# Attention stages computed with a second, turned score product in place of transposed probabilities

## The chip, the cores and the metric

The kernel runs on one core of one Trainium2 chip. The metric is the device time of one execution in microseconds. Lower is better.

## The reference, cut to what matters

The program is four layers, each a cross attention and a feed-forward part, over x of 64 sequences of 128 rows and 128 features; keys and values come from a context of 120 rows a sequence. The last layer has a self attention besides. All attention has 16 heads of 8 features. Written for one of them:

```python
h = layernorm(x)
q, k, v = (h @ Wq + bq) * 8 ** -0.5, ctx @ Wk + bk, ctx @ Wv + bv   # split into 16 heads
scores = einsum("bqhd,bkhd->bhqk", q, k)                            # masked in a2, a3 and s3
attn = softmax(scores, axis=-1)
x = x + einsum("bhqk,bkhd->bqhd", attn, v) @ Wo + bo
```

## The kernel before

x stays in on-chip memory through all stages. `build` runs them one after another, each with a barrier at its end: a0, f0, a1, f1, a2, f2, a3, a renormalisation, s3, f3. Stages a are cross attentions, s3 is the self attention (128 keys of its own rows, where the others have 120), f are feed-forward. `attention_phase` makes all attention stages. The change touches a1, a2, a3 and s3, which are its `packed` form. a2, a3 and s3 have a mask, a1 has none.

A stage handles 16 groups (NG) of four sequences (GB). A group has S = 16 slots, and in each slot one unit: four heads of one sequence. Each engine runs its own list of slots, with semaphores between them, and what a slot does is written out by hand: TensorE's slot s makes the scores of unit s, the transposes of unit s-2 (TURN), the values of unit s-4 (VALUES), and every fourth slot an output product. The projections for the next group stand in slots of this one (`slot_of`). `groups_loop` writes out the first group, turns a loop over pairs of groups, and writes out the last.

For a unit:
- `scores` (L772 to L794): one product, 96 rows of stacked queries (three terms: high, high and low part, in fp32r) as weights, 480 (or 512) columns of masked keys KM moving. With a mask, a bf16 product of the identity with the mask adds it (L792).
- `softmax_shift` on VectorE: the maximum over keys (L547), then scores minus maximum into PR (L552).
- `exponentials` on ScalarE: exp of PR in place (L704).
- `turn` on TensorE: four transposes of PR into TP (L801), which `turned` on ScalarE copies to PT (L710).
- `values` on TensorE (L825): keys are now in rows, and 16 small products in a layout of 32 columns give four heads' sums with V (VM) and their denominators (DM), into ND. VectorE takes reciprocals (L560) and normalises (L566), TensorE multiplies by Wo (L839), VectorE adds to x (L575).

For a group: `high_part` (ScalarE) and `low_part` (GpSimd, L459) split q and k. SP's queue stacks them with 24 copies within on-chip memory (L398, L404), and `masked_keys` (GpSimd, L348) spreads the stacked keys over the four heads of a unit with zeros elsewhere.

The few names that the prediction uses: PJ is the accumulator of the projections, SC of the scores, TP of the transposes.

## Time and profile before

| | |
|---|---|
| median of 3 runs | 4263.11 us (4260.68 to 4274.32) |
| profiled execution, its own time | 4260.05 us |
| its span, first to last instruction | 4258.2 us |
| TensorE, VectorE, ScalarE, GpSimd busy | 83%, 79%, 55%, 37% |
| mean granted clock of TensorE | 0.897 |
| stage a1, from its first instruction | 549.5 to 1031 us |
| stages a2 and a3 | 1377.6 to 1901.9, 2494 to 3003 us |
| stage s3 | 3034 to 3598.9 us |

Engines in the rows: PE is TensorE, PEld its loading of weights, DVE VectorE, ACT ScalarE, POOL GpSimd, SP the queue that issues most copies. Products are pipelined: a row's duration of 0.27 us for a product of 128 columns holds its latency, and the next one starts earlier than it ends. What a product costs is therefore read from the distance between starts. A row's busy share is that of its engine in the stretch. `<-` names what ended an idle time; "issue" means nothing that the profile shows.

### The profile page before, as it was taken

The page shows a single profiled execution, that of the slowest core. Times are in us where ns is not written, and L with a number is a line of the kernel's source. Part 1 is how long each engine was busy: PE and PEld are TensorE (multiplying, and loading weights), DVE is VectorE, ACT ScalarE, POOL GpSimd, SP SyncE. Part 2 cuts the span into 40 slices and gives each one's busy share as a digit, 9 for nine tenths or more (in the row PEclk, how much of TensorE's full clock was granted, in tenths as well). Part 3 has the DMA queues.
Part 4 walks back from the last instruction along what each step waited for, and adds up shares of the span by engine and source line. Part 5 has one row for each costly group of instructions (what it writes and reads, how often), then busy time and mean ns, then how long its engine had stood idle before and what let it go on. Part 6 is the DMA issues. An engine that isn't in the chain of part 4 may idle for free. (4 is left out here: it accounts for less than half of the span.)

```text
span 4258.2 us, 95393 instructions
## 1 busy us (share of the span) xinstructions
PE 3539.6 (83%) x31830; PEld 2463.6 (58%) x31831; DVE 3346.6 (79%) x6141; ACT 2332.4 (55%) x4244; POOL 1570.1 (37%) x911
## 2 busy tenths in 40 slices
PE   6983979999599899993058849999499998799999
PEld 3552646667476566662046626666365666677777
DVE  7888879998898788885035578888687877788888
ACT  2432657775376566651035536777566665466665
POOL 2210045553000454533744435554254443222222
PEclk9985989998699899995579969999699999799999
DMA  1002122222000222220112142221221112100000
GB/s 63 16 31 103 76 61 64 62 65 63 13 0 6 63 60 57 60 69 13 52 56 62 57 123 62 58 60 49 69 50 47 46 47 73 40 13 12 15 15 15
DMA packets 158984, 209.04 MB, mean 49 GB/s; under 512 B 37820, under 2 KB 109824, under 8 KB 155585
## 3 DMA queue, kind: packets, MB, share of 16 engines
q1 hardware_dynamic: 150593, 189.40, 16.4%
q0 software_dynamic: 8192, 16.92, 1.2%
q8 instruction: 132, 2.16, 0.2%
q14 instruction: 67, 0.55, 0.0%
HBM read 53.09 MB, written 42.21 MB: 22 GB/s over the span
## 5 line engine op out<-in xcount | busy, mean ns | idle before, releaser
L704 ACT ACTIVATE a_p<-a_p 128x480 f32<-128x480 f32 x832 | 501.8, 603 | 517.7 <-DVE a_p L552 515.2
L348 POOL TENSOR_TENSOR a_km<-a_k,a_slots 96x1920 fp32r<-96x1920 f32 x186 | 631.9, 3416 | 176.9 <-DMA a_k<-a_kh 176.9
L547 DVE TENSOR_REDUCE a_mx<-a_sc 128x4 f32<-128x480 f32 (+1 forms) x832 | 542.6, 652 | 124.4 <-PE a_sc L792 95.1
L552 DVE TENSOR_TENSOR a_p<-a_sc,a_mx 128x480 f32<-128x480 f32 x832 | 531.4, 639 | 18.8
L710 ACT ACTIVATE a_pt<-a_tp 120x512 f32<-120x512 f32 x832 | 487.7, 586 | 81.6 <-PE a_tp L801 76.6
L801 PE MATMUL a_tp<-ident,a_p 128*120 128x128 f32 x3328 | 509.7, 276 | 4.1 <-ACT a_p L704 2.3
L801 PEld LDWEIGHTS a_tp<-ident,a_p 128*120 128x120 f32 x3328 | 399.6, 138 | 90.0 <-ACT a_p L704 27.5
L786 PE MATMUL a_sc<-a_km,a_qr 96*128 96x480 f32 x768 | 395.1, 514 | 32.3 <-DMA a_qr<-a_ql 29.4
L825 PE MATMUL a_nd<-a_pt,a_vm 120*32 120x128 f32 x6656 | 354.6, 285 | 0.0
L825 PE MATMUL a_nd<-a_pt,a_dm 120*32 120x128 f32 x6656 | 334.4, 273 | 0.0
L1767 ACT ACTIVATE f_s<-f_pu 128x512 f32<-128x512 f32 x256 | 153.4, 599 | 212.6 <-PE f_pv L1249 212.6
L547 DVE TENSOR_REDUCE s_mx<-s_sc 128x4 f32<-128x512 f32 x256 | 176.4, 689 | 98.1 <-PE s_sc L792 97.5
L560 DVE RECIPROCAL a_rd<-a_nd 128x128 f32<-128x128 f32 x256 | 242.6, 948 | 6.7 <-PE a_nd L825 6.5
L348 POOL TENSOR_TENSOR s_km<-s_k,s_slots 96x2048 fp32r<-96x2048 f32 x62 | 224.0, 3633 | 52.2 <-DMA s_k<-s_kh 52.2
L704 ACT ACTIVATE s_p<-s_p 128x512 f32<-128x512 f32 x256 | 161.2, 630 | 146.3 <-DVE s_p L552 144.8
L1653 POOL TENSOR_TENSOR f_ya<-f_ya,f_yg 128x512 f32<-128x512 f32 x96 | 125.0, 1302 | 302.4 <-DVE f_yg L1703 302.3
L1678 DVE TENSOR_TENSOR f_a<-f_s,f_pv 128x512 f32<-128x512 f32 x256 | 175.3, 685 | 76.2 <-ACT f_s L1767 68.6
L1690 DVE TENSOR_TENSOR f_al<-f_a,f_ah 128x512 fp32r<-128x512 f32 x256 | 229.2, 895 | 0.0
L786 PEld LDWEIGHTS a_sc<-a_km,a_qr 96*128 96x128 f32 x768 | 146.0, 190 | 137.6 <-issue 128.8
L825 PEld LDWEIGHTS a_nd<-a_pt,a_vm 120*32 120x32 f32 x6656 | 131.2, 108 | 141.6 <-issue 132.3
L2078 PE MATMUL f_px<-ident,f_xr 128*128 128x128 f32 x128 | 25.0, 328 | 226.1 <-DMA f_xr<-dispatched 226.1
L825 PEld LDWEIGHTS a_nd<-a_pt,a_dm 120*32 120x32 f32 x6656 | 199.1, 110 | 0.0
(429 smaller groups left out, 8911.6 us busy)
## 6 DMA issues: line engine op xcount, KB each, us to landing
a_qr<-a_qh SPq DMA_DIRECT2D x384, 64.0 KB, 2.0
a_k<-a_kh SPq DMA_DIRECT2D x384, 60.0 KB, 2.0
a_ctx<-in_ctxT SPq DMA_DIRECT2D x64, 240.0 KB, 2.7
a_qr<-a_ql SPq DMA_DIRECT2D x192, 64.0 KB, 2.0
a_k<-a_kl SPq DMA_DIRECT2D x192, 60.0 KB, 2.0
dispatched<-f_empty SPq DMA_DIRECT2D x8, 1040.0 KB, 21.1
f_xr<-dispatched SPq DMA_DIRECT2D x32, 260.0 KB, 2.6
chosen<-f_none SPq DMA_DIRECT2D x8, 1024.0 KB, 11.9
```

Source lines behind the costliest of these rows:

```text
L348: v.tensor_tensor(KM[par][:, i, :, :].rearrange("p b (j k) -> p b j k", k=KN), K3[:, i, :, :].unsqueeze(2).to_broadcast([TR, GB, 4, KN]), ...
L547: v.tensor_reduce(mx[:], view, AX.X, ALU.max).then_inc(mx_ready, 1)
L552: v.tensor_tensor(PR[s % 4][:].rearrange("p (h k) -> p h k", k=k), view, mx[:].unsqueeze(2).to_broadcast([P, heads, k]), ALU.subtract).the ...
L560: v.reciprocal(RD[:], ND[bt % 2][:, 1, :]).then_inc(rd_ready, 1)
L704: a.activation(PR[s % 4][:], PR[s % 4][:], ACT.Exp).then_inc(exp_ready, 1)
L710: a.activation(PT[s % 4][0:KN, :], TP[s % 2][0:KN, :], ACT.Copy).then_inc(pt_ready, 1)
L786: last = t.matmul(SC[s % 2][:, 0:W], queries, keys, start=True, stop=not masked)
L801: last = t.transpose(TP[s % 2][0:KN, q * P:(q + 1) * P], PR[s % 4][:, q * KN:(q + 1) * KN], R.ident[:])
L825: last = t.matmul(ND[j % 2][32 * q:32 * q + 32, what, :], w, PT[s % 4][0:KN, q * P:(q + 1) * P], start=(what == 0 and i == 0), stop=(i == ...
L1678: v.tensor_tensor(A[s % 2][:], S[s % 2][:], PV[s % 2][:], ALU.mult).then_inc(Z["a_ready"], 1)
L1690: v.tensor_tensor(AL[s % 4][:], A[s % 2][:], AH[s % 4][:].bitcast(F32), ALU.subtract).then_inc(Z["lo_ready"], 1)
L1767: a.activation(S[s % 2][:], PU[s % 2][:], ACT.Silu).then_inc(Z["s_ready"], 1)
```

## The change

Stages a1, a2, a3 and s3 are made by a new function. For a unit the scores are formed twice. The first pass, with queries in rows, is only for the maximum: four products, one a head, each with 96 rows of masked queries QM as weights and 120 (128) columns of stacked keys KS moving. VectorE takes the maximum of each (into MX, 16 columns a sequence). Once a sequence, TensorE transposes MX, VectorE negates it into NEG, and ScalarE's queue copies NEG into row 96 of QM. The second pass has keys in rows: KS with a row of ones as 97th is the weights, and QM with the row of minus the maximum is moving, 512 columns, so that the product is score minus maximum and already turned. ScalarE takes exp from the accumulator ST straight to PT. Masked stages add the mask in both passes, in the second from its transpose `addm_t`. The subtraction, the transposes of probabilities and the copy of these are gone.

Keys are no longer masked; queries are (`masked_queries`). The stacking goes by way of memory: high and low parts are written there (`part_out`), and each of the three terms is read back in one copy (`stack_up`). The lags between slots are longer (second pass 9, values 11, output 14 slots behind the first), three groups are written out ahead of the loop, and SP's list is written out whole. Projections stand in slots 2, 4, 6 and 10.

```diff
+def turned_attention_phase(nc, R, I, name, wq, wk, wv, wo, bq=None, bk=None, bv=None, bo=None, own_keys=False, mask=None,
+                           causal=None, ln=None):
...
+    TR = 3 * 32
+    KR = TR + 1
+    U = 4
+    S = GB * U
+    LN_SLOTS = (0, 0, 0, 1)
+    SUM_SLOT, STATS_SLOTS = 14, (15, 15, 15, 15)
+    TURN, NEGATE, WEIGH, VALUES, RECIP, OUTPUT = 5, 6, 9, 11, 12, 14
+    KN = P if own_keys else KC
+    W = 4 * KN
+    steps_of = ["ht", "q", "k", "v"]
+    slot_of = dict(zip(steps_of, (2, 4, 6, 10)))
...
+        KS = [sb(n_(f"ks{i}"), [KR, U, GB, KN], F32R) for i in range(2)]
+        QS = sb(n_("qs"), [TR, U, GB, P])
+        QM = [sb(n_(f"qm{i}"), [KR, GB, U, 4, P], F32R) for i in range(2)]
...
+        MX = [sb(n_(f"mx{i}"), [P, 16]) for i in range(2)]
+        NEG = [sb(n_(f"neg{i}"), [16, P], F32R) for i in range(2)]
...
+        SC = [ps(n_(f"sc{i}"), [P, 512]) for i in range(2)]
+        ST = [ps(n_(f"st{i}"), [P, 512]) for i in range(2)]
...
+                def part_out(step, g, par, which, part):
+                    buffer = R.parts[step][par, which, :, 0:part.shape[1]]
+                    sp.dma_start(buffer, part[:].bitcast(F32)).then_inc(parts_out[step], 16)
+                def stack_up(step, g, par, out, cols_of, order):
+                    sp.wait_ge(parts_out[step], 32 * (g + 1))
+                    for term, which in enumerate(order):
+                        src = R.parts[step][par, which, :, 0:cols_of].rearrange("(i r) c -> r i c", r=32)
+                        sp.dma_start(out[32 * term:32 * term + 32], src).then_inc(stack_in[step], 16)
+                def stack_terms(g, par):
+                    sp.wait_ge(high_ready["q"], g + 1)
+                    part_out("q", g, par, 0, HIGH["q"])
+                    sp.wait_ge(low_ready["q"], g + 1)
+                    part_out("q", g, par, 1, LOW["q"])
+                    sp.wait_ge(high_ready["k"], g + 1)
+                    part_out("k", g, par, 0, HIGH["k"])
+                    sp.wait_ge(low_ready["k"], g + 1)
+                    part_out("k", g, par, 1, LOW["k"])
+                    at_least(sp, qm_ready, g * GB)
+                    stack_up("q", g, par, QS[:].rearrange("p i b t -> p i (b t)"), GT, (0, 0, 1))
+                    at_least(sp, st_ready, (g - 1) * S)
+                    stack_up("k", g, par, KS[par][:].bitcast(F32).rearrange("p i b k -> p i (b k)"), W, (0, 1, 0))
...
+                for g in range(NG):
+                    if not own_keys and 1 <= g < NG - 1:
+                        ctx_load(g + 1, (g + 1) % 2)
+                    stack_terms(g, g % 2)
...
+                def masked_queries(g, par, b):
+                    at_least(pool, st_ready, (g - 2) * S + (b + 1) * U)
+                    nc.gpsimd.tensor_tensor(QM[par][0:TR, b, :, :, :],
+                                            QS[:, :, b, :].unsqueeze(2).to_broadcast([TR, U, 4, P]),
+                                            slots[:].unsqueeze(1).unsqueeze(3).to_broadcast([TR, U, 4, P]),
+                                            ALU.mult).then_inc(qm_ready, 1)
+                def prepare(g, par):
+                    low_part("q", g)
+                    low_part("k", g)
+                    pool.wait_ge(stack_in["q"], 48 * (g + 1))
+                    for b in range(GB):
+                        masked_queries(g, par, b)
+                prepare(0, 0)
+                groups_loop(pool, lambda g, par, first, last: None if last else prepare(g + 1, 1 - par), 3)
...
+                def maxima(g, s):
+                    n = g * S + s
+                    j, i = s // U, s % U
+                    dve.wait_ge(sc_ready, n + 1)
+                    if i == 0:
+                        at_least(dve, mt_ready, g * GB + j - 1)
+                    v.tensor_reduce(MX[j % 2][:, 4 * i:4 * i + 4], SC[s % 2][:, 0:W].rearrange("p (h k) -> p h k", k=KN), AX.X,
+                                    ALU.max).then_inc(mx_ready, 1)
...
+                def negated(b, bt):
+                    dve.wait_ge(mt_ready, b + 1)
+                    if not isinstance(b, int) or b >= 2:
+                        dve.wait_ge(neg_in[bt % 2], (b - bt % 2) * 8)
+                    v.tensor_scalar(NEG[bt % 2][:], ND[(bt + 1) % 2][0:16, 2, :], -1.0, None, ALU.mult).then_inc(neg_ready, 1)
...
+                def negated_in(b, bt, par):
+                    act.wait_ge(neg_ready, b + 1)
+                    act.dma_start(QM[par][TR:KR, bt, :, :, :].rearrange("p i j t -> p (i j t)").bitcast(F32),
+                                  NEG[bt % 2][:].bitcast(F32)).then_inc(neg_in[bt % 2], 16)
+                def exponentials(g, s):
+                    n = g * S + s
+                    act.wait_ge(st_ready, n + 1)
+                    at_least(act, pv_done, n - 3)
+                    a.activation(PT[s % 4][0:KN, :], ST[s % 2][0:KN, :], ACT.Exp).then_inc(exp_ready, 1)
+                def behind(g, s, par, first):
+                    if s - WEIGH < S and not (first and s < WEIGH):
+                        exponentials(g, s - WEIGH)
+                    u = s - NEGATE
+                    if u % U == 0 and u < S and not (first and u < 0):
+                        negated_in(g * GB + u // U, (u // U) % GB, par if u >= 0 else 1 - par)
...
+                def scores(g, s, par):
+                    n = g * S + s
+                    j, i = s // U, s % U
+                    if i == 0:
+                        pe.wait_ge(qm_ready, g * GB + j + 1)
+                    if s == 0:
+                        pe.wait_ge(stack_in["k"], 48 * (g + 1))
+                    at_least(pe, mx_ready, n - 1)
+                    if masked:
+                        t.matmul(SC[s % 2][:, 0:W], R.ident_bf[:], addm[:].unsqueeze(1).to_broadcast([P, 4, KN]), start=True,
+                                 stop=False, skip_group_check=True)
+                    for h in range(4):
+                        last = t.matmul(SC[s % 2][:, h * KN:(h + 1) * KN], QM[par][0:TR, j, i, h, :], KS[par][0:TR, i, j, :],
+                                        start=not masked, stop=True, skip_group_check=True)
+                    last.then_inc(sc_ready, 1)
+                def weigh(g, s, par):
+                    n = g * S + s
+                    j, i = (s // U) % GB, s % U
+                    if i == 0:
+                        b = g * GB + s // U
+                        pe.wait_ge(neg_in[j % 2], (b + 2 - j % 2) * 8)
+                    at_least(pe, exp_ready, n - 1)
+                    last = t.matmul(ST[s % 2][0:KN, :], KS[par][:, i, j, :],
+                                    QM[par][:, j, i, :, :].rearrange("p h t -> p (h t)"), start=True, stop=not masked)
+                    if masked:
+                        last = t.matmul(ST[s % 2][0:KN, :], R.ident_bf[0:KN, 0:KN],
+                                        addm_t[0:KN, :].unsqueeze(1).to_broadcast([KN, 4, P]), start=False, stop=True)
+                    last.then_inc(st_ready, 1)
+                def values(g, s, par, last):
+                    n = g * S + s
+                    j, i = (s // U) % GB, s % U
+                    if s % S == 0:
+                        pe.wait_ge(ready["v"], g + s // S + 1)
+                    pe.wait_ge(exp_ready, n + 1)
+                    if i == 0:
+                        at_least(pe, ct_ready, g * GB + s // U - 1)
+                        if not (last and s // U == GB - 1):
+                            pe.wait_ge(neg_ready, g * GB + s // U + 2)
+                    for what in range(2):
+                        for q in range(4):
+                            h = 4 * q + i
+                            w = DM[0:KN, i, :] if what else VM[par][0:KN, j, 32 * h:32 * h + 32]
+                            last = t.matmul(ND[j % 2][32 * q:32 * q + 32, what, :], w,
+                                            PT[s % 4][0:KN, q * P:(q + 1) * P],
+                                            start=(what == 0 and i == 0), stop=(i == U - 1), skip_group_check=True,
+                                            tile_position=(0, 32 * q))
+                    last.then_inc(pv_done, 1)
+                def maxima_turn(b, bt):
+                    pe.wait_ge(mx_ready, b * U + U)
+                    at_least(pe, ct_ready, b - 2)
+                    t.transpose(ND[(bt + 1) % 2][0:16, 2, :], MX[bt % 2][:], R.ident[:]).then_inc(mt_ready, 1)
...
+                def behind(g, s, par, first, last):
+                    if s - WEIGH < S and not (first and s < WEIGH):
+                        weigh(g, s - WEIGH, par if s >= WEIGH else 1 - par)
+                    if s - VALUES < S and not (first and s < VALUES):
+                        values(g, s - VALUES, par if s >= VALUES else 1 - par, last)
+                    u = s - TURN
+                    if u % U == 0 and u < S and not (first and u < 0):
+                        maxima_turn(g * GB + u // U, (u // U) % GB)
+                    u = s - OUTPUT
+                    if (u + 1) % U == 0 and u < S and not (first and u < 0):
+                        gg = g if u >= 0 else g - 1
+                        output(gg, g * GB + u // U, (u // U) % GB)
...
+                def group(g, par, first, last):
+                    for s in range(S):
+                        scores(g, s, par)
+                        behind(g, s, par, first, last)
+                        if not last:
+                            for step in steps_of:
+                                if slot_of[step] == s:
+                                    project(step, g + 1, 1 - par)
+                    if last:
+                        for s in range(S, S + OUTPUT):
+                            behind(g, s, par, False, True)
...
+        R.parts = {w: nc.dram_tensor(f"parts_{w}", [2, 2, P, GT], F32).ap() for w in "qk"}
...
-        attention_phase(nc, R, I, "a1", I["L1_xattn_wq"], I["L1_xattn_wk"], I["L1_xattn_wv"], I["L1_xattn_wo"],
-                        I["L1_xattn_bq"], I["L1_xattn_bk"], I["L1_xattn_bv"], I["L1_xattn_bo"])
+        turned_attention_phase(nc, R, I, "a1", I["L1_xattn_wq"], I["L1_xattn_wk"], I["L1_xattn_wv"], I["L1_xattn_wo"],
+                               I["L1_xattn_bq"], I["L1_xattn_bk"], I["L1_xattn_bv"], I["L1_xattn_bo"])
...
```

a2, a3 and s3 are called in the same way. The parts left out set up tiles, projections, evictions, reciprocals and the sum into x, as before in kind.

## Rows read from the trace of the kernel before

**Rows 1.** Busy time by stretch, a1 and a3: from:to, length, busy (instructions) by engine, granted clock.
```profile
600.00:1000.00 400.00, 395.73 (x5185) 270.35 (x5175) 377.39 (x715) 286.33 (x529) 230.03 (x87) 1.00 0.26 63
...
2530.00:2980.00 450.00, 449.82 (x5629) 297.30 (x5617) 385.58 (x726) 315.95 (x566) 234.08 (x88) 1.00 0.23 57
```

**Rows 2.** The same view for the maxima of line 547 alone: a1, a2, a3.
```profile
600.00:1000.00 400.00, 148.80 (x230) 1.00 0.26 63
1430.00:1880.00 450.00, 154.57 (x237) 1.00 0.23 57
2530.00:2980.00 450.00, 156.51 (x240) 1.00 0.23 57
```

**Rows 3.** Timeline of VectorE, three sums into x in s3: start, us, instruction.
```profile
3173.89 0.68 DVE L575 TENSOR_TENSOR x<-x,s_out 128x512 f32 x1
...
3205.01 0.68 DVE L575 TENSOR_TENSOR x<-x,s_out 128x512 f32 x1
...
3242.15 0.68 DVE L575 TENSOR_TENSOR x<-x,s_out 128x512 f32 x1
```

**Rows 4.** Timeline of TensorE, one unit of s3 and the next one's start.
```profile
3301.34 0.48 PE L786 MATMUL s_sc<-s_km,s_qr 96*128 96x512 f32 x1
3301.66 0.39 PE L792 MATMUL s_sc<-s_addm,ident_bf 128*128 128x512 bf16 x1
3301.89 0.60 PE L801 MATMUL s_tp<-ident,s_p 128*128 128x128 f32 x4
3302.42 0.43 PE L825 MATMUL s_nd<-s_pt,s_vm 128*32 128x128 f32 x8
...
3302.99 0.50 PE L786 MATMUL s_sc<-s_km,s_qr 96*128 96x512 f32 x1
```

**Rows 5.** Timeline of TensorE in a1: scores and the transposes behind them.
```profile
802.87 0.49 PE L786 MATMUL a_sc<-a_km,a_qr 96*128 96x480 f32 x1
803.20 0.49 PE L801 MATMUL a_tp<-ident,a_p 128*120 128x128 f32 x3
```

**Rows 6.** Transposes, ns min/median/max; and the timeline's eight products of the v projection in a3.
```profile
L801 PE MATMUL s_tp<-ident,s_p x1024: 272/273/421, 3065.2 to 3592.0; 128*128 128x128 f32 x171
...
2601.49 1.14 PE L763 MATMUL a_pj<-a_wv,a_ctx 128*120 128x128 f32 x8
```

**Rows 7.** Timeline of TensorE in f3: fp32r products of 512 columns in a row.
```profile
3681.61 0.39 PE L1245 MATMUL f_pu<-f_xh,f_w1hi 128*128 128x512 f32 x1
3681.83 0.39 PE L1246 MATMUL f_pu<-f_xh,f_w1lo 128*128 128x512 f32 x1
```

**Rows 8.** The page's costliest groups: busy us, mean ns | idle before, and its end.
```profile
L348 POOL TENSOR_TENSOR s_km<-s_k,s_slots 96x2048 fp32r<-96x2048 f32 x62 | 224.0, 3633 | 52.2 <-DMA s_k<-s_kh 52.2
L547 DVE TENSOR_REDUCE a_mx<-a_sc 128x4 f32<-128x480 f32 (+1 forms) x832 | 542.6, 652 | 124.4 <-PE a_sc L792 95.1
L552 DVE TENSOR_TENSOR a_p<-a_sc,a_mx 128x480 f32<-128x480 f32 x832 | 531.4, 639 | 18.8
L710 ACT ACTIVATE a_pt<-a_tp 120x512 f32<-120x512 f32 x832 | 487.7, 586 | 81.6 <-PE a_tp L801 76.6
L560 DVE RECIPROCAL a_rd<-a_nd 128x128 f32<-128x128 f32 x256 | 242.6, 948 | 6.7 <-PE a_nd L825 6.5
```

**Rows 9.** Loop turn in s3; one pass of the loop in a3 and s3; instruction packets in s3's.
```profile
3156.40 0.79 PE L786 MATMUL s_sc<-s_km,s_qr 96*128 96x512 f32 x1 [3.62 <-issue]
...
2726.00:2786.30 60.30, 60.27 (x753) 39.80 (x752) 51.76 (x99) 42.39 (x76) 31.83 (x12) 1.00 0.24 59
3220.50:3288.70 68.20, 64.66 (x756) 41.68 (x755) 53.98 (x99) 43.78 (x76) 33.55 (x13) 0.95 0.20 48
...
q8 instruction: 9, 0.15, 1.0%
```

**Rows 10.** First scores of a1 (timeline); the page's stacking copies, KB each, us to landing.
```profile
578.96 0.74 PE L786 MATMUL a_sc<-a_km,a_qr 96*128 96x480 f32 x1 [9.95 <-DMA a_qr<-a_ql]
...
a_k<-a_kh SPq DMA_DIRECT2D x384, 60.0 KB, 2.0
```

354 lines of the change are left out of this document (347 added, 7 removed).

## The prediction

> **What bounds the kernel now.** I read the busy shares by stage first, then the cadence of the units, then one unit of TensorE in order of time. The change touches four stages, a1, a2, a3 and s3, each of 16 groups of 16 units (a unit is four heads of one sequence), 1024 units in all. In the steady stretch of a3 the reader is to see TensorE busy for 449.82 of 450 us at granted clock 1.00, while VectorE has 385.58 [rows 1]. In a1 both are near full: TensorE 395.73 of 400, VectorE 377.39 [rows 1]. The maxima come once a unit and so count units: 230 in 400 us, 237 in 450, 240 in 450, which is 1.74, 1.90 and 1.88 us a unit, or 27.8, 30.4 and 30.0 us a group [rows 2]. In s3 two sums into x stand 31.12 us apart, and the next two 37.14 [rows 3]; the 6.0 us between them are a stall (below).
>
> One unit of s3 by its starts: scores 0.32, mask 0.23, four transposes 0.53, values 0.57, 1.65 us together [rows 4]; nothing idles in it. The unit of a1 without a mask is 0.33 for the scores [rows 5] and, with the same two pieces, 1.43. So TensorE sets a2, a3 and s3, by what it issues; a1 runs 16 x 1.43 = 22.9 us of units in a group of 27.8, of which some 4.1 us are projections and outputs (16 units of 1.63, s3's less 0.02 for 32 columns fewer, leave 3.9 of a3's 30.0 and 4.3 of a2's 30.4) and some 0.8 us is waiting on the softmax chain. What counts is therefore TensorE's time per unit before and after.
>
> **What is taken off other engines.** The subtraction (639 ns) leaves VectorE, the copy of the turned probabilities (586 ns) leaves ScalarE [rows 8]. VectorE would then have per group 16 maxima at 0.65, four reciprocals at 0.95 [rows 8] and some 4 us of small work (normalising, layer norm, statistics, four negations): 18 us of 30. ScalarE has 16 exponentials and six evictions of the copy's length, the back-to-back ones 0.1 shorter, and four DMA issues: some 15. GpSimd masks queries in place of keys, four times 3.63 us, as 96x2048 shows [rows 8], and two small subtractions: some 17 us, an estimate. None of them ends last, so this removal is worth only a1's 0.8 us of waiting a group. Cover: if one of them fell behind by more than 12 us a group it would show.
>
> **TensorE, step by step.** Price of a small product: where 128-column products each bring their own weights, eight of them take 1.14 us with the last lasting 0.27, so they start (1.14-0.27)/7 = 0.12 us apart, the first one's load included; four transposes of 273 ns take 0.60, so (0.60-0.273)/3 = 0.109 [rows 4, 6]. A transpose streams 128 columns, 0.05 us at the rate of the 512-column product (one start per 0.22 us [rows 7]), so 0.11 is the loading of weights.
> - Removed: four transposes, 4 x 0.11; the 0.53 they take ends with 0.15 in which nothing starts, the change to the 32-column layout of the values. The 0.15 stays, behind whatever stands there.
> - The wide score product becomes four, 96x128 queries as weights and 120 (128) keys moving, in fp32r. The trace has fp32r only 480 and 512 wide. Lower bound: 0.05 apart (the stream alone); upper bound: the plain f32 price, two records of 0.11 for a 128-column product, 0.20 at 120 columns. I take 0.11, since the operation of the same shape that also loads 128 weights is the nearest row; fp32r weights load in about that too (scores: 0.33 less 0.20 of streaming, 0.13 [rows 5]).
> - Added: the second pass, 97x120 weights, 512 columns: load 0.11, stream 0.22. Added in a2, a3, s3: a second mask product, 0.23 [rows 4]. Values stay, 0.57.
> - Unit with mask: mask 0.23 (the first load hides under it), four starts 0.44 (the last is the load of the second pass), stream 0.22, mask 0.23, change of layout 0.15, values 0.57: 1.84 against 1.65, +0.19. Without mask: exposed load 0.11, 0.44, 0.22, 0.15, 0.57: 1.49 against 1.43, +0.06.
> - Turn of the maxima: one small transpose per sequence, load and stream 0.16, four a group, 0.65. Negation and its DMA (issued by ScalarE at slot 6, wanted at slot 9) have three units, 5 us, against 2.0 us to landing for the present stacking copies [rows 10].
> - Sum by group: a2, a3, s3: 16 x 0.19 + 0.65 = 3.7; a1: 16 x 0.06 + 0.65 - 0.8 = 0.8. Sum by stage: a1 +13, a2 +59, a3 +59, s3 +59: +190.
>
> The Trainium skill (TensorE: Matmul & The Clock Gate, "Back-to-back issue gap") gives a sustained 81 ns for a pair of weight load and 128-column product. The transposes show 109 ns, so the measurement decides; by the page the sum would be 1024 x 4 x 0.028 = 115 us less, still a slower kernel. The case is a rival below.
>
> **Stalls at the turn of a loop.** In s3 TensorE stops for 3.62 us for no releaser when its loop turns, and the next products run at the lower clock: 0.79 where 0.48 is usual [rows 4, 9]. A pass of a3's loop takes 60.3 us with TensorE busy for 60.27, one of s3's 68.2 with 64.66, for 753 and 756 products; in s3's the queue for instructions brings 9 packets [rows 9], in a3's none. So s3's loop doesn't stay in the engine's instruction store and a3's does; which, I take it, hangs on where its start falls in a block. Six turns, 36 us, are in s3 now. The change makes the loops of a2, a3, s3 longer (23 products a unit for 22, and four turns a group: some 5%), so more of them may not fit; peeling three groups leaves five turns. I take two of the three stalling: 2 x 5 x 6.0 = 60, less 36: +24. Bounds: none stalls, -36; all four, +84.
>
> **Preparation and ends.** Queries and keys are stacked by way of memory: 4 writes and 6 reads on SP's queue a group in place of 24 copies, each write and read taken at 2.0 us to land [rows 10]. Behind SP's wait for the written parts stand the stacked queries, behind these GpSimd's masking and the first scores of the next group. The last low part is done about slot 8, the stack lands about slot 11, the first masked block is there at slot 13 and is wanted at slot 16: hidden, with 5 us to spare. At a stage's start nothing hides it: in a1 the first scores start at 578.96, after 9.95 us in which TensorE waited for the last stacking copy [rows 10]; one more trip through memory and queries masked at 3.63 us per four units cost some 6 us, and the masking of the first keys, of about that length, is gone. I take +3 a stage, +12; from 0 to +40.
>
> **Sum.** Against the profiled execution's own 4260.05 us (span 4258.2; the median of the runs shown is 4263.11, so 3 us lie between them): 4260 + 190 + 24 + 12 = 4486 us.
>
> **Rivals.**
> - *fp32r of 120 columns at the price of plain f32.* Each product 0.20 (s3 0.21) in place of 0.11: 768 x 4 x 0.09 + 256 x 4 x 0.105 = +386: 4872. For: no row shows fp32r narrower than 480, and plain f32 is cut in two records. Against: wide fp32r goes in one record at the rate of bf16 [rows 4, 7]. The Trainium skill (FP8 and Floating Point Precision, "TensorE Precision Notes") gives four passes to true fp32 and reads reduced fp32 truncated, so it ties the passes to the precision and not to the width, which speaks against this rival; no run so far shows it.
> - *Preparation ends late.* If the trip through memory or a wait in SP's queue takes over 5 us more than I give it, TensorE waits for masked queries at each group's start. At 2 us by 64 groups: +128, 4614.
> - *The loads hide in part.* Half way between the stream's 0.05 and the load's 0.11, at 0.08, each small product saves 0.03: 4096 x 0.03 = 123 us, 4363. For: loads run on a queue of their own. Against: a run of four or of eight with one spacing throughout [rows 4, 6]. The page's 81 ns, above, speaks for this case.
> - *Faster than before.* The sum has +226 to lose over 4096 small products: from a spacing of 0.055 us down, that is when the load of the 128 weights hides wholly behind 50 ns of streaming, the change wins. With 0.05, 4096 x 0.059 = 242 us less: 4244; if the 0.15 of layout change went as well, 4090. For: only that loads and products are separate queues. Against: transposes at 0.11.
> - *It doesn't relieve what it says.* It does, but of engines that don't bind; that is in the forecast, not beside it.
>
> **How the numbers follow.** Forecast 4486: 0.45 (its own range 4410 to 4560: stalls and ends). Plain f32 price 0.27. Late preparation 0.12. Loads hidden in part 0.09. Faster 0.05. 0.02 is left for others. The range 4350 to 4890 leaves out the faster case and tails. What a measurement can tell from no change is about 0.3%, 13 us: faster 0.05, same 0.02, slower 0.93.
>
> **What would show it.** In the profile after: a masked unit of 1.84 us from score to score, with TensorE still busy throughout and VectorE near 60%; four score products 0.11 apart (0.20: the first rival; under 0.06: the last); 0.22 for the second pass; a group of 33.7 us in a3 and 28.6 in a1. Gaps of 3.6 us with "issue" as their end at loop turns count the stalls. Wrong would be: TensorE idle before the first scores of a group, ended by GpSimd (late preparation) or by a DMA (negated maxima late); a granted clock under 1.00 in steady stretches; or VectorE or ScalarE ending most waits.

## The result, and the profile after

The changed kernel takes 4749.25 us (median of 4 runs, 4740.25 to 4770.65) against 4262.05 us before: 1.114 times as long, interval 1.110 to 1.119. It is slower, as forecast, and inside the range, but by 487 us where 226 were forecast.

The time is all in the four stages that were changed. From the first maxima of a stage to its last (255 units, from the starts of L547 and L1141) the two profiled executions, with spans of 4258.2 and 4768.8 us (the second is the slowest of the four runs), give:

| stage | before, us | after, us | difference | forecast, products and maxima | usual group, before | usual group, after |
|---|---|---|---|---|---|---|
| a1 | 442.5 | 646.4 | +203.9 | +13 | 27.9 | 37 to 45 |
| a2 | 481.8 | 594.8 | +113.0 | +59 | 30.45 | 34.7, five of 41 to 44 |
| a3 | 477.8 | 586.8 | +109.0 | +59 | 30.15 | 34.7, five of 40 to 42 |
| s3 | 527.9 | 560.6 | +32.7 | +59 - 36 | 31.1, stalls 37 | 35.0 |

The other 52 us of the 510.6 between the spans lie at the beginnings and ends of these stages.

The first view is busy time by stretch, as in [rows 1]: from:to, length, then PE, PEld, DVE, ACT and POOL with their instructions, granted clock, DMA share, GB/s. The stretches are in a1, a3 and s3 of the kernel after.

```profile
650.00:1150.00 500.00, 465.52 (x4484) 316.49 (x4476) 266.50 (x470) 153.48 (x257) 209.81 (x75) 0.70 0.26 68
2900.00:3350.00 450.00, 415.08 (x4706) 273.58 (x4706) 240.52 (x441) 154.22 (x263) 203.35 (x73) 0.95 0.30 77
3600.00:4050.00 450.00, 437.57 (x5108) 295.26 (x5106) 278.12 (x479) 169.36 (x283) 216.56 (x78) 1.00 0.29 75
```

Before, TensorE was busy for 449.82 of 450 us in a3 at 1.00 [rows 1]. Now it stands for 35 of 450, and in a1 the granted clock is 0.70. VectorE has fallen from 385.58 to 240.52 us, as the change intended, and no time came of it.

One masked unit of a3, the timeline of TensorE in the kernel after, answers to [rows 4]: start, us, instruction.

```profile
3001.02 0.38 PE L1358 MATMUL a_sc<-a_addm,ident_bf 128*128 128x480 bf16 x1
3001.05 0.73 PE L1361 MATMUL a_sc<-a_ks,a_qm 96*128 96x120 f32 x4
3001.62 0.44 PE L1373 MATMUL a_st<-a_qm,a_ks 97*120 97x512 f32 x1
3001.90 0.38 PE L1376 MATMUL a_st<-a_addm_t,ident_bf 120*120 120x512 bf16 x1
3002.21 0.43 PE L1396 MATMUL a_nd<-a_pt,a_vm 120*32 120x128 f32 x8
3002.45 0.40 PE L1396 MATMUL a_nd<-a_pt,a_dm 120*32 120x128 f32 x8
3002.79 0.38 PE L1358 MATMUL a_sc<-a_addm,ident_bf 128*128 128x480 bf16 x1
...
3004.45 0.50 PE L1373 MATMUL a_st<-a_qm,a_ks 97*120 97x512 f32 x1 [0.90 <-DMA a_qm<-a_neg]
```

It takes 1.77 us from mask to mask, where 1.84 was forecast. The four small products in fp32r start 0.112 us apart, as plain transposes do. The price of the products was therefore near, and the loss must come from the stops, of which the last row shows one, and in a1 from the clock. The waits of TensorE over the whole kernel after (us in total, times, longest; the waits in other stages are left out):

```profile
PE a_pj L1327 <- DVE a_h L151: 87.6, 29, 15.2
...
PE a_sc L1358 <- POOL a_qm L1067: 39.7, 8, 9.8
...
PE a_st L1373 <- DMA a_qm<-a_neg: 38.2, 38, 2.2
PE s_pj L1327 <- DVE s_h L151: 27.1, 16, 7.8
```

The first and the last are for rows h of the layer norm. Between the first and the last maxima of a1, a2, a3 and s3 they come to 31, 17, 19 and 25 us; in a2 and a3 most of that is in two early groups, with stops of 7.8 and some 5 us, and a later group loses 1.3 us at most. Timelines of VectorE and GpSimd in a3 show why they come late:

```profile
2865.72 8.59 DVE L151 TENSOR_SCALAR a_h<-x,a_mean,a_rstd 128x128 f32<-128x128 f32 x3
2874.23 0.65 DVE L1141 TENSOR_REDUCE a_mx<-a_sc 128x4 f32<-128x480 f32 x1
2874.80 0.33 DVE L151 TENSOR_SCALAR a_h<-x,a_mean,a_rstd 128x128 f32<-128x128 f32 x1
```
```profile
2859.95 14.27 POOL L1067 TENSOR_TENSOR a_qm<-a_qs,a_slots 96x2048 fp32r<-96x2048 f32 x4 [6.20 <-DMA a_qs<-parts_q]
```

Three rows of L151 take 8.59 us while GpSimd masks queries; the fourth, begun after GpSimd's end at 2874.22, takes 0.33. Over all 256 instructions of L151 in the kernel after, the 175 that start outside a masking take 0.33 us in the mean and the 81 that start inside one 2.69, at most 3.77. The maxima, which read PSUM, take 0.66 us in either case. Not every read of SBUF is held up: the statistics of x, read from SBUF, take 0.26 us inside a masking and 0.27 outside, and the sums into x 0.68 in either case. Before, one L151 of 240 started inside a masking: VectorE wrote rows at slots 1 and 2 (in s3 at slot 0), when GpSimd's masking of keys was over. The sign was there all the same: 43 of the 240 ran beside GpSimd's subtraction (L459) and took up to 1.28 us. The masking of queries now runs over the turn of the group. The Trainium skill (SBUF — State Buffer, "SBUF: two separate sides") says that VectorE and GpSimd share a pair of ports, which one instruction locks for its whole length while the other blocks; of VectorE's operations it names those in a mode with two ports and those with two inputs in SBUF. The times of L151 agree, though no row shows in which mode it runs, and the rule should have been weighed when GpSimd's work was moved.

The second stop is a turn of TensorE's loop, here in a3 of the kernel after; it answers to [rows 9]:

```profile
3044.03 0.40 PE L1396 MATMUL a_nd<-a_pt,a_dm 120*32 120x128 f32 x8
3047.64 0.37 PE L1358 MATMUL a_sc<-a_addm,ident_bf 128*128 128x480 bf16 x1 [3.21 <-issue]
```

There are five of these in a2, five in a3 and none in s3: the count that was forecast for two masked stages. The view puts only four of the ten down to "issue" and six to the masked queries, as here:

```profile
3111.49 14.27 POOL L1067 TENSOR_TENSOR a_qm<-a_qs,a_slots 96x2048 fp32r<-96x2048 f32 x4 [7.82 <-DMA a_qs<-parts_q]
```
```profile
3122.96 0.37 PE L1358 MATMUL a_sc<-a_addm,ident_bf 128*128 128x480 bf16 x1 [3.48 <-POOL a_qm L1067]
```

But these scores need only the first of the four maskings, which had ended 7.9 us before them and some 4 us before the stop began, and with the loop written out (e4 below) the waits for masked queries within the stages are gone but for one of 0.2 us. The other two of the 8 waits of the row above (L1358, 39.7 us) are the starts of a2 and a3. The third is the copy of the negated maxima. Issues of DMA in a3, 2900 to 3350 us (KB each, median us from issue to landing), and in a stretch of 2 us of a1:

```profile
a_qs<-parts_q SPq DMA_DIRECT2D x36, 256.0 KB, 4.4
a_ks<-parts_k SPq DMA_DIRECT2D x36, 240.0 KB, 6.3
...
a_qm<-a_neg ACTq DMA_DIRECT2D x48, 8.0 KB, 1.8
```
```profile
a_ks<-parts_k SPq DMA_DIRECT2D x3, 240.0 KB, 6.2
a_qm<-a_neg ACTq DMA_DIRECT2D x1, 8.0 KB, 6.4
```

The copy of 8 KB lands in 1.8 us as a rule, but in 6.4 when it is issued beside the stacking reads; the forecast gave it 5 us of slack.

### The profile page after: what moved, and what is told of

Read it like the earlier page. It is cut to its first block and busy times, and to the rows that moved or that the text cites. A ratio compares the mean times of both kernels' runs of the same rounds, so it can differ in the third digit from the quotient of the medians.

```text
span 4768.8 us, 93410 instructions
## 1 busy us (share of the span) xinstructions
PE 3901.0 (82%) x32858; PEld 2726.1 (57%) x32858; DVE 3003.1 (63%) x5376; ACT 1812.8 (38%) x3220; POOL 1622.4 (34%) x919
## 5 line engine op out<-in xcount | busy, mean ns | idle before, releaser
L1141 DVE TENSOR_REDUCE a_mx<-a_sc 128x4 f32<-128x480 f32 x768 | 502.2, 654 | 644.1 <-PE a_sc L1361 643.8
L1281 ACT ACTIVATE a_pt<-a_st 120x512 f32<-120x512 f32 x768 | 457.6, 596 | 997.0 <-PE a_st L1376 651.4
L1067 POOL TENSOR_TENSOR a_qm<-a_qs,a_slots 96x2048 fp32r<-96x2048 f32 x192 | 685.2, 3599 | 320.7 <-DMA a_qs<-parts_q 301.0
L1361 PE MATMUL a_sc<-a_ks,a_qm 96*128 96x120 f32 x3072 | 635.3, 336 | 10.2 <-POOL a_qm L1067 10.0
L1361 PEld LDWEIGHTS a_sc<-a_ks,a_qm 96*128 96x128 f32 x3072 | 525.3, 223 | 105.4 <-issue 86.5
L1373 PE MATMUL a_st<-a_qm,a_ks 97*120 97x512 f32 x768 | 389.2, 507 | 38.4 <-DMA a_qm<-a_neg 38.2
L1141 DVE TENSOR_REDUCE s_mx<-s_sc 128x4 f32<-128x512 f32 x256 | 176.2, 688 | 203.1 <-PE s_sc L1361 203.1
L1067 POOL TENSOR_TENSOR s_qm<-s_qs,s_slots 96x2048 fp32r<-96x2048 f32 x64 | 228.4, 3599 | 103.0 <-DMA s_qs<-parts_q 103.0
L1281 ACT ACTIVATE s_pt<-s_st 128x512 f32<-128x512 f32 x256 | 152.4, 595 | 274.4 <-PE s_st L1376 274.1
L1358 PE MATMUL a_sc<-a_addm,ident_bf 128*128 128x480 bf16 x512 | 199.9, 390 | 52.9 <-POOL a_qm L1067 39.7
L1376 PE MATMUL a_st<-a_addm_t,ident_bf 120*120 120x512 bf16 x512 | 201.9, 394 | 0.0
```

Of the source, the lines that this page charges most:

```text
L1067: nc.gpsimd.tensor_tensor(QM[par][0:TR, b, :, :, :], QS[:, :, b, :].unsqueeze(2).to_broadcast([TR, U, 4, P]), slots[:].unsqueeze(1).unsque ...
L1141: v.tensor_reduce(MX[j % 2][:, 4 * i:4 * i + 4], SC[s % 2][:, 0:W].rearrange("p (h k) -> p h k", k=KN), AX.X, ALU.max).then_inc(mx_ready, 1)
L1281: a.activation(PT[s % 4][0:KN, :], ST[s % 2][0:KN, :], ACT.Exp).then_inc(exp_ready, 1)
L1358: t.matmul(SC[s % 2][:, 0:W], R.ident_bf[:], addm[:].unsqueeze(1).to_broadcast([P, 4, KN]), start=True, stop=False, skip_group_check=True)
L1361: last = t.matmul(SC[s % 2][:, h * KN:(h + 1) * KN], QM[par][0:TR, j, i, h, :], KS[par][0:TR, i, j, :], start=not masked, stop=True, skip_ ...
L1373: last = t.matmul(ST[s % 2][0:KN, :], KS[par][:, i, j, :], QM[par][:, j, i, :, :].rearrange("p h t -> p (h t)"), start=True, stop=not masked)
```

## The experiments

All times are medians; the interval, where it matters, is that of the ratio to the kernel before. "Core" is the time from first to last maxima of a stage.

**A mask of zeros in a1** (e1_fill_a1):

```diff
-    masked = mask is not None or causal is not None
+    masked = mask is not None or causal is not None or fill
...
+                if fill:
+                    nc.gpsimd.memset(addm[:], 0.0).then_inc(filled, 1)
+                    nc.gpsimd.memset(addm_t[:], 0.0).then_inc(filled, 1)
...
```

> The changed kernel, whose unmasked stage a1 now issues the two mask products a unit that a2 and a3 issue, with an additive mask of zeros, so what is computed stays the same and only work is added. Theory of the clock (a1 lost most because its units, which bring nearly as many weight loads as before but fewer streamed columns, run at 0.70 of the clock): with the added columns a1 keeps the clock as a2 and a3 do, its unit falls from 2.56 us to about 1.8, and the stage from 700 us to 600 to 640 us; the kernel comes to some 4650 to 4690 us in place of 4749. Rival, the waits alone (negated maxima, rows of the layer norm) make a1 long and the low clock is only their mark: the added products lengthen a1 by 256 units x 0.35 us = 90 us, to some 790 us, and the kernel comes to 4840.

Measured: 4719.92 us, 30 over the upper expectation. The core of a1 fell from 646.4 to 592.0 us with 512 products more, and the same stretch of a1 now reads:

```profile
650.00:1150.00 500.00, 467.98 (x5320) 308.07 (x5313) 275.45 (x511) 166.83 (x280) 228.71 (x82) 0.95 0.29 75
```

So the clock, not the waits alone, made a1 long: TensorE's waits in its core are 44.6 us now and were 51.4. The total fell by 29 us only, since the stalls of the loop's turn moved: a3 had none (core 554.6, groups of 34.5), a1 and s3, which had none, now had five each, and a2 kept its five (core 609.4, 15 us more). In s3 (core 590.9, 30 more):

```profile
3637.58 0.40 PE L1400 MATMUL s_nd<-s_pt,s_dm 128*32 128x128 f32 x8
3641.42 0.60 PE L1362 MATMUL s_sc<-s_addm,ident_bf 128*128 128x512 bf16 x1 [3.44 <-issue]
```

s3's loop is the same code in both kernels, some 190 products further on in TensorE's list.

**No copies of negated maxima** (e2_no_neg):

```diff
+                for t in QM:
+                    v.tensor_scalar(t[TR:KR, :, :, :, :].rearrange("p b i h t -> p (b i h t)"),
+                                    R.ones[TR:KR, 0:1].to_broadcast([1, GB * U * 4 * P]), 0.0, None, ALU.mult).then_inc(ones_row, 1)
...
-                    act.dma_start(QM[par][TR:KR, bt, :, :, :].rearrange("p i j t -> p (i j t)").bitcast(F32),
-                                  NEG[bt % 2][:].bitcast(F32)).then_inc(neg_in[bt % 2], 16)
...
-                        pe.wait_ge(neg_in[j % 2], (b + 2 - j % 2) * 8)
...
```

> The changed kernel without the copies of the negated maxima into row 96 of the queries: that row stays zero, so the maximum is not subtracted, and ScalarE issues 1024/4 fewer copies; the first pass, the maxima, their turn and the negation all stay. Theory that the copies landing late hold TensorE (in the trace after it waited 82 us for them in the four stages, 0.9 to 2.2 us at a time): each of a2, a3 and s3 falls by 10 to 25 us, and a1 by more, 40 to 100 us, because each wait there is followed by units at the lower clock; the kernel comes to 4600 to 4680 us. Rival, those waits cover others that end nearly as late (the softmax chain, the masked queries): under 20 us in all, 4730 or more.

Measured: 4759.65 us, no gain; the first theory missed in the total. (The 82 us that it starts from are 38.2 in the rows of a stages above, and 0.6 in s3.) By stage it did better: a1's core fell by 45 us to 601.3, a2 and a3 by 12 and 1, and s3 took the loop's stalls (599.3, +39). The edit also brings work of its own. VectorE zeroes row 96 at the start of each stage, here of a1, and the parts outside the cores are 25 us longer than in the changed kernel:

```profile
554.51 8.76 DVE L1090 TENSOR_SCALAR a_qm<-ones 1x8192 fp32r<-1x8192 f32 x2
```

The waits for rows h grew from 87.6 to 166.4 us, most of it in a1's core, from 31.2 to 85.6:

```profile
PE a_pj L1326 <- DVE a_h L151: 166.4, 38, 19.3
```

In a1 the waits for copies had covered part of those for the rows. The total of this run is a sum of gains, of stalls that moved and of the edit's own cost, and says little about the copies; the stages have to be read one by one.

**Rows h by ScalarE** (e3_h_act):

```diff
+                v.scalar_tensor_tensor(hshift[:], norm.mean[:], -1.0, norm.rstd[:], ALU.mult, ALU.mult).then_inc(hshift_ready, 1)
...
-                    ins = norm.apply_one(dve, g, j, H)
...
+                    ins = a.activation(H[:, j, :], R.x[:, b, :], ACT.Identity, scale=norm.rstd[:, bass.ds(b, 1)],
+                                       bias=hshift[:, bass.ds(b, 1)])
...
```

> The changed kernel with the normalised rows h written by ScalarE (scale and bias per row) in place of VectorE, nothing else. Theory that VectorE's four operations a group stand behind GpSimd's masking of the queries (up to 3.6 us each where 0.7 is usual) and so hold TensorE's projections (117 us of waits in the attention stages, 27 in s3): the waits for h are gone, each stage falls by 10 to 35 us, a1 by most; kernel 4640 to 4700 us. Rival, ScalarE has no room and the waits move from h to the exponentials: 4740 to 4780.

Measured: 4606.53 us, 143 less, and more than was expected. Cores: a1 554.5, a2 568.1, a3 564.9, s3 535.6. The waits for h are gone (87.6 us and 27.1 before, where the expectation has 117 and 27), and the second group of a3, 43.6 us before, takes 33.4. One row takes ScalarE 0.48 us. The cores fell by 92 us in a1 and by 27, 22 and 25 in the others: the largest gain of any one edit to the changed kernel, though in a2 and a3 the next edit gives as much.

**Loops written out** (e4_straight):

```diff
-                groups_loop(pe, group, 3)
+                for g in range(NG):
+                    group(g, g % 2, g == 0, g == NG - 1)
```

> The changed kernel with TensorE's loop over groups written out in the four turned stages, the same products in the same order. Theory that the stalls at the loop's turn come from fetching instructions: the long groups of a2 and a3 (five each of 40.4 to 44.4 us beside 34.7) fall to 34.7, which is 5 x 6.5 us or some 30 to 35 us a stage, a1 and s3 show no change (under 5 us); kernel 4680 to 4690 us. Rival, a straight list must be fetched throughout and stalls everywhere: each stage as long as now or longer, 4750 or more.

Measured: 4727.56 us. The cores of a2 and a3 fell by 24 and 25 us and the alternate long groups are gone. The rest of the expectation missed: a1 fell by 36, though its waits did not get less (55.5 us for 51.4), which stays open. s3 rose by 14, with 14 waits of 0.8 to 7.8 us, 28.3 in all, the first products of a group waiting for h, and no stall with issue as its end. A list without a loop is not held up by fetching. In a2 and a3 the waits for h grew from 17.4 and 19.1 to 29.7 and 30.5 us: the stalls had covered some of them.

**The kernel before with s3 written out** (e6_before_straight_s3), the same edit in s3 alone:

> The kernel before, with TensorE's loop over groups written out in s3 alone, the same products in the same order. Theory of the prediction (six stalls of 6.0 us there come from fetching instructions at the loop's turn): every group of s3 takes 31.1 us and the kernel comes to some 4227 us, 36 us or 0.8% less. Rival, a list that never repeats has to be fetched throughout, so that stalls come at other places: 4250 to 4290.

Measured: 4230.70 us against 4263.79, ratio 0.991, interval 0.990 to 0.993. Every group of s3 but the first takes 31.1 us, its core 492.3 for 527.9, and TensorE never stands:

```profile
3100.00:3500.00 400.00, 400.00 (x4852) 259.11 (x4849) 346.34 (x631) 278.30 (x490) 214.92 (x78) 1.00 0.22 52
```

It is the fastest kernel of this study and beats both. That the stall belongs to the loop's turn is shown; that it is fetching is argued from the packets of the queue for instructions alone, and the list written out brings 7 such packets in 68 us of s3 (3150 to 3218) without a stop.

**Three causes out at once** (e7_h_fill_straight): rows h by ScalarE, loops written out, a1 filled.

> The changed kernel with three things at once: rows h written by ScalarE, the loops of TensorE written out in the four turned stages, and the two mask products a unit with a mask of zeros in a1. Theory that what the forecast missed is these three (VectorE's rows behind GpSimd, the loop's turn, the clock of a1), and that its price of the products held: the groups of a1, a2 and a3 all take 33 to 34 us and those of s3 34 to 35, from first to last maxima 500 to 515 us in a1, a2 and a3 and 530 to 550 in s3; the kernel comes to 4430 to 4480 us, beside 4486 forecast. Rival, another limit (the copies of the negated maxima, the softmax chain) takes their place: groups stay at 36 us or more, kernel over 4560.

Measured: 4499.91 us, ratio 1.054 (1.051 to 1.056), 20 over the upper expectation. After the first, groups take 33.0 to 34.6 us in a1, a2 and a3 and 33.8 to 35.2 in s3; a1 and a3 both run at 1.00. (The cores, 527 to 530 in the a stages, are longer than the 500 to 515 that I put; without the waits for the copies of the maxima, in e10 below, they are 513 to 519.)

```profile
700.00:1100.00 400.00, 393.30 (x4700) 261.39 (x4699) 209.66 (x404) 162.85 (x289) 197.33 (x70) 1.00 0.31 79
2850.00:3200.00 350.00, 344.55 (x4141) 228.63 (x4140) 178.98 (x344) 146.72 (x263) 167.58 (x60) 1.00 0.32 81
```

**One small product of four** (e8_one_product), on top of that:

```diff
-                    for h in range(4):
+                    for h in range(1):
                         last = t.matmul(SC[s % 2][:, h * KN:(h + 1) * KN], QM[par][0:TR, j, i, h, :], KS[par][0:TR, i, j, :],
```

> The last kernel (rows h by ScalarE, written-out loops, filled a1) with only the first of the four small score products of the first pass in every unit of the four stages: the maxima of three heads in four are those of the mask alone, and 3072 products of 96x128 weights with 120 or 128 columns are left out. Theory of the prediction, that such a product costs what its weights take to load, 0.11 us by the trace after: each unit loses 3 x 0.112 = 0.34 us, a group 5.4 us, each stage 86 us and the kernel 344 us against the last one. Rival, something beside TensorE already ends nearly as late: under 200 us less. Second rival, plain f32 price: 600 us less.

Measured: 4310.73 us, 189 less: the rival's number. But the shortest groups take 27.6 us in a3, where 33.0 less 5.4 is 27.6, so the price holds wherever nothing else ends last. Elsewhere the waits for the copies came forward:

```profile
PE a_st L1383 <- DMA a_qm<-a_neg: 76.5, 39, 3.5
```

It is still no faster than before, without 3072 of its products.

**The kernel before with rows h by ScalarE too** (e9_before_h_act), and s3 written out:

> The kernel before with s3's loop written out and, in all stages with 16 units a group, rows h of the groups after the first written by ScalarE in place of VectorE. Theory that a1 has 0.8 us a group in which TensorE waits for the softmax chain of VectorE (377 of 400 us busy): a1 falls by up to 13 us and the other stages do not move, some 4213 us. Rival, ScalarE's added operations come between an exponential and the copy of its turned probabilities and delay those: 0 to 30 us more than the kernel with s3 alone written out.

Measured: 4266.36 us, 36 us more than e6. a1's core went from 443.2 to 441.4 us: taking the rows off VectorE does not remove a1's few tenths of idle time a group. s3 lost 37 us: there the first products of every group wait up to 1.9 us for h from ScalarE, 27.2 us in all. The edit helps only where VectorE's rows collide.

**Clean loops, a1 as the change made it** (e11_h_straight): e7 without the mask of zeros.

> The kernel of the last call with rows h by ScalarE and the loops written out, but without the added mask products in a1, so a1 is as the change made it. Theory of the clock: TensorE's waits for rows h are gone and yet the unmasked stage runs with a granted clock under 0.9, units of 2.58 us beside units of 1.43; a1 takes 34 us or more a group, 540 to 580 us from first to last maxima, and the kernel comes to 4510 to 4560 us, slower than with the mask products of zeros (4500). Rival, the clock was lost only to the long waits for h: a1 runs at 1.00 with groups of 28.6 to 30 us, some 440 us, and the kernel comes to some 4410.

Measured: 4556.68 us; a1's core 590.0, with a granted clock of 0.75 from 650 to 1120 us. Timeline of TensorE in a1:

```profile
893.52 0.66 PE L1367 MATMUL a_sc<-a_ks,a_qm 96*128 96x120 f32 x4
894.02 0.44 PE L1379 MATMUL a_st<-a_qm,a_ks 97*120 97x512 f32 x1
...
894.96 0.66 PE L1367 MATMUL a_sc<-a_ks,a_qm 96*128 96x120 f32 x4
898.16 0.78 PE L1379 MATMUL a_st<-a_qm,a_ks 97*120 97x512 f32 x1 [2.55 <-DMA a_qm<-a_neg]
...
900.35 1.09 PE L1367 MATMUL a_sc<-a_ks,a_qm 96*128 96x120 f32 x4
901.23 0.73 PE L1379 MATMUL a_st<-a_qm,a_ks 97*120 97x512 f32 x1
```

A unit takes 1.44 us up to the wait, and 2.58 after it, for unit after unit with no further wait; the granted clock is back at 1.00 at 931, 34 us after it fell. Not every stop does this: one of 1.50 us, at 983, left it at 1.00.

**Clean, and no copies of maxima** (e10_no_neg_clean): e7 with the edit of e2.

> The kernel with rows h by ScalarE, written-out loops and filled a1 (4500 us), without the copies of the negated maxima: row 96 stays zero, so the maximum is not subtracted. Theory that with the larger waits gone these copies are what is left over the products: the waits of TensorE for them (28 us in four stages) are gone and the kernel falls by 25 to 40 us, to 4460 to 4475, groups of 33.2 us throughout. Rival, they still cover something else: under 10 us.

Measured: 4471.85 us, 28 less than e7; after the first two groups every group takes 33.2 us in a1 and a2, 33.0 in a3, 33.8 in s3. The edit pays for its zeroing here too: outside the cores the stages are 25 us longer than in e7, and the four cores together fell by 50 us, where e7 has 28 us of waits for these copies in them.

**Clean, with small stacking reads** (e5b_small_stack):

```diff
                 def stack_up(step, g, par, out, cols_of, order):
+                    if g >= 3:
+                        cols_of, out = 4, out[:, :, 0:4]
```

> The same kernel (4500 us) with, from the fourth group on, the stacking reads from memory cut to 4 columns in place of 480 to 512, so that scores are computed of old data from then on; the number of copies and every wait stay. Theory that the copy of the negated maxima issued at slot 10 lands late (6.4 us for 1.8) because it stands behind the large stacking reads in the same 16 DMA engines: all these copies land in 1.8 to 2.2 us, the waits of TensorE for them are under 3 us in four stages, kernel 20 to 35 us less. Rival, it is the count of copies in flight or ScalarE that issues late: the waits stay at 25 us.

Measured: 4459.12 us, 41 less than e7, with the copies of the maxima all still there and no wait of TensorE for them after the first groups. The groups are those of e10. Of the 256 copies 59 take over 5 us to land in e7 and 6 here, though some 40 still take around 3 us. So it is the large reads beside them that make these copies late. The gain, 6 us over the upper expectation, is in the cores, which fell by 43 us together.

**Clean, small reads, a1 without the mask** (e12_h_straight_small): e11 with that edit.

> The kernel with rows h by ScalarE and the loops written out, a1 without the mask products of zeros (4557 us), and with the stacking reads cut to 4 columns from the fourth group on (scores of old data from then on), so that no wait for negated maxima is left. It parts two theories of a1's low clock. Theory one: a wait of TensorE of some microseconds drops the clock and the unmasked units can't raise it again; without waits a1 runs at 1.00 with units of 1.44 us, groups of 28 to 29 us as forecast, some 440 us from first to last maxima, and the kernel comes to 4380 to 4400 us. Theory two: the stream of unmasked units itself can't hold the clock; units of 2.58 us stay in the stage, which takes 500 us or more, kernel 4450 or more.

Measured: 4382.11 us, ratio 1.027 (1.025 to 1.029). Theory one holds, except that a stop of 1.23 us is enough. a1's core is 456.0, groups of 27.2 us after the third. The first three still have whole reads and take 29.5, 43.5 and 34.9 us; the stop falls there, at 646, and the clock is at 1.2 GHz from it to 670. Stretches of a1, a3 and s3, and one unit of a1:

```profile
750.00:1030.00 280.00, 280.00 (x3777) 197.41 (x3776) 178.67 (x352) 140.80 (x251) 168.07 (x61) 1.00 0.15 47
2650.00:3050.00 400.00, 400.00 (x4815) 266.33 (x4808) 207.65 (x400) 175.60 (x316) 201.10 (x73) 1.00 0.13 40
3300.00:3700.00 400.00, 400.00 (x4723) 271.32 (x4722) 210.69 (x394) 170.49 (x301) 190.28 (x68) 1.00 0.10 32
```
```profile
880.07 0.66 PE L1369 MATMUL a_sc<-a_ks,a_qm 96*128 96x120 f32 x4
880.57 0.44 PE L1381 MATMUL a_st<-a_qm,a_ks 97*120 97x512 f32 x1
880.94 0.42 PE L1404 MATMUL a_nd<-a_pt,a_vm 120*32 120x128 f32 x8
881.18 0.40 PE L1404 MATMUL a_nd<-a_pt,a_dm 120*32 120x128 f32 x8
881.51 0.28 PE L1414 MATMUL a_nd<-ident,a_mx 128*16 128x128 f32 x1
```

From 670 us on nothing stops the unmasked stream, and it stays at 2.4 GHz to the end of the stage's last scores.

## Why the prediction was right and wrong

The experiments give a ledger from 4749 to 4262 us: rows h behind GpSimd 143 (e3), loop turns 50 (e11 against e3), large reads in front of the copies of the maxima, with the low clock that follows their waits in a1, 175 (e12 against e11), and 120 us that are left when TensorE hardly stands any more (e12 against before). Of the 175, 134 are in a1's core by the profiled runs. The 120 are a net amount: some 122 for what TensorE issues in a group, 40 outside the cores, and 36 less for the stalls that s3 had before. The order of removal matters, as e4 shows, so the three amounts are those of this order.

- **What bounds the kernel, and that the removal is worth nothing.** Right. Outside the loop turns of s3 TensorE waited for 6 us in the four cores before, VectorE's and ScalarE's relief bought nothing in the masked stages, and e8 shows how far the added products are from free.
- **Price of the products.** Right in kind, and high by a third. e12 has the sum alone. Masked units take 1.77 for 1.84 us: 0.60 from the mask to the second pass, 0.28 to its mask, 0.31 to the values and 0.58 to the next mask, where the sum has 0.67, 0.22, 0.38 and 0.57. Unmasked ones take 1.44 for 1.49. That is 768 x 0.07 + 256 x 0.05 = 67 us too much in +190. By groups e12 has a2 33.2 for 30.45, a3 33.0 for 30.15, s3 33.8 for 31.1, and a1 27.2 for 27.9: in a1 the change is a small gain per group. 16 groups give 44 + 46 + 43 - 11 = +122, which is 190 less 67.
- **Plain f32 price, loads that hide, faster.** All three rivals fell: the spacing of 120-column fp32r products is 0.112 us, where 0.20, 0.08 and 0.055 had been needed. A fp32r product of 120 or 128 columns has one record, while each of the four plain f32 products of the v projection has two ([rows 6] counts eight records, and the values are likewise 8 products in 16 records). The Trainium skill (TensorE: Matmul & The Clock Gate, "Back-to-back issue gap") has 81 ns for a pair of load and 128-column product, which these 112 ns do not bear out. (The first rival's +386 adds up to 384.)
- **Stalls at the loop's turn.** Right in kind and in number (five each in two of three stages). That it hangs on where the loop lies is shown by e1, where s3's unchanged loop begins to stall and a3's ceases to; e6 shows the cost of s3's, 33 us in the median, 36 in the core.
- **Preparation and ends.** Forecast +12, up to +40. In e12 the parts outside the cores are 40 us longer than before (2.3, 7.7, 12.0, 7.9 and 10.4 us, from the start of the kernel to its end): the upper bound. The changed kernel itself has 52, beyond it.
- **Negation and its DMA: 5 us of slack against 2.0 us.** This step failed. I took the landing time of the stacking copies before, 60 KB each; the change itself puts six reads of 240 to 256 KB beside the copy in each group, and it then takes 6.4 us. e5b and e10 show the cost where the clock is kept, 43 and 50 us of the cores, and e12 against e11 what it is with the clock that a1 loses, 175.
- **"None of them ends last."** This step failed too, and by most. I summed each engine's busy time and found room (18 us of 30 for VectorE), and did not ask what GpSimd's 14.3 us of masking does to VectorE, though the change puts it where VectorE writes h. There L151 takes 2.69 us in the mean for 0.33, and e3, which gives these rows to ScalarE, gains 143 us. Slowed operations, not a full engine, made VectorE late.
- **Granted clock taken as 1.00.** Wrong in a1, where it was 0.70. It is a consequence of the stops: e12, without them, has 1.00 from 670 us on, and e11, with waits of up to 2.8 us, 0.75. Masked units got it back in a few (6.8 us after a stop of 3.21 in a3), unmasked ones did not until the projections or later (34 us in e11). So stops of much the same sum, 51 and 45 us, go with far more time in a1 (+204) than in a3 (+109).

The rival "preparation ends late" (4614) did not come true: within the stages TensorE never stood for masked queries, the first of which are there 4 to 5 us before each stop at a loop's turn (the prediction has 5 to spare), while it stood for h 45 times. That the measured time lies between this rival and the plain f32 price (4872) is chance.

## What to carry to other kernels

When work is moved to another slot or queue, ask not only whether its engine has time but what runs beside it there: VectorE's scaling of rows in SBUF beside a long GpSimd operation, a small transfer that a critical wait needs beside large ones. When several waits of like size end close together, remove them together before judging one: copies, mask of zeros and loops gave +10, -29 and -22 us singly, and rows h, loops and small reads together 367 of the change's 487. Count what the edit itself adds, and read an experiment by stage: the +10 hold 25 us of zeroing and 39 of stalls that moved. Where TensorE's loop shows gaps that nothing releases, write out that loop: it gave 0.9% in the kernel before, for no change of the work.

## What was not expected of the hardware

- VectorE's 128x128 TENSOR_SCALAR from SBUF takes 0.33 us alone and up to 3.77 us when begun during a GpSimd operation of 3.6 us; reductions from PSUM (0.66 us) and statistics from SBUF (0.26 us) don't change.
- In a1, a stop of 2.55 us took TensorE from 2.4 to 1.2 GHz (unit 1.44 to 2.58 us) and one of 1.23 us did so too, while one of 1.50 us did not; and adding 512 products of zeros to the stage made its core 54 us shorter, with the granted clock going from 0.70 to 0.95.
- An 8 KB copy takes 1.8 us to land, or 6.4 us beside reads of 240 KB. With these reads cut to 2 KB TensorE waits for it no more.
- Which loop of TensorE stalls changes with edits elsewhere: 3.1 to 3.9 us a turn and the low clock after it, in s3 before, in a2 and a3 after, in a1, a2 and s3 in e1. Written out, none does.
